# Moving the second half's residual additions behind the numbered rows, and pairing the updates of the third phase

## The chip, the cores and the metric

The program runs on one core of a Trainium2 chip. The metric is the time of one execution in device microseconds; several timed executions are given by their median. The engines are named as in the profile: PE (TensorE), DVE (VectorE), ACT (ScalarE), POOL (GpSimd) and SP (SyncE, which here only issues transfers). Each runs its own instruction list in order, and a semaphore wait in that list holds up everything behind it on that engine.

## The reference, cut to what matters

Eight sequences of 512 tokens with 128 channels go through two layers. The first three blocks (attention, a gated token mix, linear attention with a memory and three MLP levels) take the first 550 us and aren't touched by the change, apart from the residual that they leave in `X`. The change lies in the last block, a router with eight experts and two iterations:

```python
h = layernorm(x)                       # xf below: the block's own input
topk_p, topk_i = top_k(softmax(gelu(xf @ router_w1) @ router_w2), 2)
v, integrated = 0, xf
for _ in range(2):                                   # iterations it = 1, 2
    ctx = concat([integrated, v])
    x_sh, v_sh = _inl(gelu(ctx @ shared_w1) @ shared_w2, integrated, v, mu)
    x_r, v_r = sum over the 2 chosen experts of topk_p * _inl(gelu(ctx @ w1[e]) @ w2[e], ...)
    x_next, v_next = sw * x_sh + (1 - sw) * x_r, sw * v_sh + (1 - sw) * v_r
    integrated = integrated + halt * (x_next - integrated)
    v = v + halt * (v_next - v)
refined = gelu(integrated @ refine_w1) @ refine_w2
out = x + (xf + integration_weight * refined)        # the residual of this block
```

The two additions of the last line are where `X` comes in: the kernel adds the normed input to the residual early (`X += xnb`), and the refined part at the end.

## The kernel before, in words

**Tiles and halves.** A token tile is 128 tokens by 128 channels; a sequence has four. Sequences 0 to 3 are half 0, sequences 4 to 7 half 1. `xnb[t]` is the normed input of sequence t, `Y1[t]` is `xnb[t] - mu`, and `X` is the residual. For half 0 `xnb` lies in `LX`, for half 1 in 2,048 columns of `TEMP` that the expert inputs `XS` use later.

**Routing by slots.** After the router, a half's tokens are sorted by expert into 40 tiles of slots (`sort(h)` on DVE, 20-odd small instructions; its last, line 1123, counts `so_pos`). POOL then writes each token row twice, once for each of its two experts, to the slots in DRAM, with indirect DMAs of 128 rows. For half 0 that is `scatter(0, m)`: 32 DMAs on line 675. For half 1 the rows carry a number in a 129th column, so these 32 DMAs are the numbered rows (`numbered(k, m)`, line 684): 16 for the first expert, a wait and a small instruction, 16 for the second. The first of them waits for `so_pos`; later ones wait for `v_el`, the count of groups that DVE has finished, at values that lag behind the rows.

**Groups.** The iterations run as 56 groups of 512 tokens or slots. An S group is the shared path of four token tiles, an E group the expert path of four slot tiles. The order is S 0 to 3 (half 0, iteration 1), E 4 to 13 (the same), S 14 and 15 and E 16 to 25 (half 1, iteration 1), S 26 and 27, S 28 to 31 and E 32 to 41 (half 0, iteration 2), S 42 to 45 and E 46 to 55 (half 1, iteration 2). Every engine loops over steps s. In step s DVE copies the gate values of group s out of PSUM (`copy_b`, line 1180), runs `elements(s - 2)` (for an S group lines 1211, 1213, 1215, 1222) and `moved_on(s - 2)` (lines 1235, 1244, 1249), and in some steps `routes`, `hots` (line 1081) or `sort` of half 1: routes(1) and hots(1) in step 2, sort(1) in step 3. The E groups of a half and iteration can only be loaded by SP (line 510) when all the rows of that half have landed in the slots.

**Updates.** What an E group gives is stored by slot. POOL gathers it back by token: `gather(ph, m)`, two indirect DMAs on line 770 into one of four buffers `G`, for the 16 tiles m of phase ph (0: half 0, 1: half 1 of iteration 1; 2: half 0 of iteration 2). DVE adds it to the tokens: `update(ph, m)`, lines 1273 and 1276, in a step that the table `UPDATES` gives. `gather(ph, m)` waits for `update(ph, m - 4)`, whose buffer it takes. In the third phase, ph 2, POOL runs step by step too: it first writes the results of E group s - 2 to their tokens (`slots_back`, four indirect DMAs on line 693, three for the last group; they wait for `v_el`), then issues `gather(2, m + 4)` for each update m that the table has for this step. So the table sets DVE's order and POOL's at once.

**The end.** When the last `slots_back` rows have landed, SP reads the rows of half 1 back (`load_tokens`, line 529), DVE makes the updates of phase 3, and PE, ACT and DVE refine the last sequences.

**Around the change.** POOL's list before the numbered rows is: 32 scatter DMAs, then `moved(1)`, which makes the four `Y1` subtractions of half 1 (line 659), the four additions `X += xnb` of half 1 (line 661) and a copy of the row numbers (line 663), then `ones_row(1)`, a memset of one partition (line 699). The same `moved(0)` runs earlier for half 0.

## Time and profile before

| | us |
|---|---|
| timed runs | 991.86, 994.6, 995.5 |
| median | 994.6 |
| the profiled execution | 991.68 |
| its span, first to last instruction | 989.9 |
| PE busy | 782.1 (79%) |
| DVE busy | 577.9 (58%) |
| ACT busy | 566.4 (57%) |
| POOL busy | 488.1 (49%) |

The 1.8 us between the profiled execution and its span lie around the instructions. The shares of busy time are averages over stages with different limits, so they don't say what a change in one stage is worth. For that one follows the chain of waits: the work that ended last, traced back step by step to what released it.

### The profile page before, as it was taken

The page shows a single profiled execution, that of the slowest core. Times are in us where ns is not written, and L with a number is a line of the kernel's source. Part 1 is how long each engine was busy: PE and PEld are TensorE (multiplying, and loading weights), DVE is VectorE, ACT ScalarE, POOL GpSimd, SP SyncE. Part 2 cuts the span into 40 slices and gives each one's busy share as a digit, 9 for nine tenths or more (in the row PEclk, how much of TensorE's full clock was granted, in tenths as well). Part 3 has the DMA queues.
Part 4 walks back from the last instruction along what each step waited for, and adds up shares of the span by engine and source line. Part 5 has one row for each costly group of instructions (what it writes and reads, how often), then busy time and mean ns, then how long its engine had stood idle before and what let it go on. Part 6 is the DMA issues. An engine that isn't in the chain of part 4 may idle for free.

```text
span 989.9 us, 13034 instructions
## 1 busy us (share of the span) xinstructions
PE 782.1 (79%) x3904; PEld 535.8 (54%) x3904; DVE 577.9 (58%) x1438; ACT 566.4 (57%) x1003; POOL 488.1 (49%) x436
## 2 busy tenths in 40 slices
PE   7799997587888877999999856575576668877477
PEld 4588886444444435767676644454344444544255
DVE  6622333648888682222434588658566877586655
ACT  5744444544445304635544539877666898788532
POOL 1411202335554486224434777537777775467750
PEclk9999999799999997999999969887898999888789
DMA  9940000000000000000000535657557664633124
GB/s 344 423 136 1 0 1 1 1 1 0 1 1 1 0 1 0 1 1 1 1 1 27 186 92 152 207 158 226 166 175 238 202 191 146 196 121 101 48 78 128
DMA packets 75921, 92.90 MB, mean 94 GB/s; under 512 B 24032, under 2 KB 61920, under 8 KB 73808
## 3 DMA queue, kind: packets, MB, share of 16 engines
q1 hardware_dynamic: 65248, 65.87, 20.7%
q0 software_dynamic: 10464, 25.66, 8.1%
q10 hardware_dynamic: 144, 0.59, 0.2%
q8 instruction: 31, 0.51, 0.2%
q14 instruction: 34, 0.28, 0.1%
HBM read 45.95 MB, written 46.13 MB: 93 GB/s over the span
## 4 chain that ended last, share of the span: by engine, by line
PE 46%; DVE 16%; POOL 11%; ACT 11%; issue 9%; DMA 5%; POOLq 0%; DVEq 0%; SPq 0%; ACTq 0%
PE PS L1945 7%; PE PS L1954 6%; POOL tokens L693 4%; POOL KEEP L770 3%; PE PS L1752 3%; PE PS L1723 3%; PE PS L1864 3%; PE PS L1960 3%; PE PS L1832 3%; POOL slots L684 3%; PE PS L1713 2%; DMA KEEP<-moved,small 2%; DVE TEMP L961 2%; PE PS L1660 2%; PE PS L2058 2%
## 5 line engine op out<-in xcount | busy, mean ns | idle before, releaser
L2069 PE MATMUL PS<-TEMP,KEEP 128*128 x320 | 116.9, 508 | 36.9 <-ACT TEMP L1569 30.4
L770 POOL DMA_INDIRECT KEEP<-moved,small x96 | 104.4, 1087 | 69.9 <-issue 35.4
L675 POOL DMA_INDIRECT slots<-KEEP,small x96 | 101.1, 1053 | 47.2 <-issue 27.4
L2069 PEld LDWEIGHTS PS<-TEMP,KEEP 128*128 128x128 f32 x320 | 66.5, 223 | 65.1 <-issue 50.7
L1509 ACT ACTIVATE KEEP<-PS,TEMP 128x512 f32<-128x512 f32 x96 | 63.5, 690 | 58.0 <-PE PS L1945 57.1
L1569 ACT ACTIVATE TEMP<-PS 128x512 f32<-128x512 f32 (+2 forms) x92 | 51.5, 561 | 78.3 <-DVE TEMP L1180 77.7
L621 POOL TENSOR_TENSOR KEEP<-KEEP 128x1024 f32<-128x1024 f32 x32 | 63.7, 2005 | 53.6 <-PE PS L1864 51.8
L1945 PE MATMUL PS<-TEMP_R 128*128 128x512 f32 x288 | 77.1, 422 | 4.2 <-POOL TEMP_R L715 3.8
L2091 PE MATMUL PS<-KEEP,TEMP 128*64 128x128 f32 x480 | 40.2, 308 | 42.2 <-issue 19.1
L1864 PE MATMUL PS<-KEEP,TEMP 128*128 128x512 f32 x128 | 62.7, 619 | 9.3 <-DVE TEMP L961 8.2
L1945 PEld LDWEIGHTS PS<-TEMP_R 128*128 128x128 f32 x288 | 56.2, 198 | 20.1 <-POOL TEMP_R L715 4.2
L1180 DVE COPY TEMP<-PS 128x256 f32<-128x256 f32 (+1 forms) x92 | 43.8, 477 | 37.9 <-PE PS L2058 19.4
L2091 PEld LDWEIGHTS PS<-KEEP,TEMP 128*64 128x64 f32 x480 | 29.7, 154 | 64.4 <-issue 25.3
L1582 ACT ACTIVATE KEEP<-PS,TEMP 64x128 f32<-64x128 f32 x160 | 57.7, 360 | 9.4 <-PE PS L2091 7.6
L1954 PE MATMUL PS<-KEEP,TEMP 128*128 128x512 f32 x128 | 56.3, 593 | 0.0
L2058 PE MATMUL PS<-WL,KEEP 128*128 128x257 f32 (+1 forms) x128 | 47.7, 510 | 6.4 <-ACT TEMP L1569 6.3
L1666 PE MATMUL PS<-WL,TEMP 128*128 128x128 f32 x256 | 39.9, 297 | 16.0 <-DMA TEMP<-slots 13.1
L1273 DVE SCALAR_TENSOR_TENSOR KEEP<-KEEP,small 128x256 f32<-128x256 f32 (+1 forms) x64 | 26.5, 414 | 39.7 <-DMA KEEP<-moved,small 33.5
L1127 DVE TENSOR_SCALAR TEMP_R<-PS,TEMP 128x512 fp32r<-128x512 f32 x16 | 12.0, 751 | 62.3 <-PE PS L1954 62.3
L961 DVE TENSOR_TENSOR TEMP<-PS,KEEP 128x1024 f32<-128x1024 f32 x32 | 38.9, 1216 | 15.0 <-PE PS L1864 13.1
L1666 PEld LDWEIGHTS PS<-WL,TEMP 128*128 128x128 f32 x256 | 31.6, 151 | 27.8 <-issue 21.0
L715 POOL TENSOR_TENSOR TEMP_R<-KEEP,TEMP_R 128x512 fp32r<-128x512 f32 x8 | 8.7, 1090 | 73.3 <-ACT KEEP L1501 73.3
(275 smaller groups left out, 1877.5 us busy)
## 6 DMA issues: line engine op xcount, KB each, us to landing
slots<-LX SPq DMA_DIRECT2D x14, 1024.0 KB, 25.8
moved<-LX SPq DMA_DIRECT2D x20, 512.0 KB, 3.3
TEMP<-slots SPq DMA_DIRECT2D x20, 512.0 KB, 3.8
TEMP<-experts SPq DMA_DIRECT2D x80, 64.5 KB
TEMP<-seconds SPq DMA_DIRECT2D x1, 3072.0 KB
TEMP<-early SPq DMA_DIRECT2D x1, 2765.0 KB, 12.0
TEMP<-experts SPq DMA_DIRECT2D x80, 32.5 KB
TEMP<-slots SPq DMA_DIRECT2D x10, 258.0 KB, 3.8
```

Of the source, the lines that this page charges most:

```text
L621: pool.tensor_tensor(o, kk, vv, ALU.mult).then_inc(S["c1_kv"], 1)
L675: pool.indirect_dma_start(dst, bass.IndirectOffsetOnAxis(ap=pos[:, h, 2 * m + k:2 * m + k + 1], axis=0), src, None).then_inc(SC[h], 16)
L770: pool.indirect_dma_start(G[:, n % 4, k, 0:w], None, src, bass.IndirectOffsetOnAxis(ap=pos[:, h, 2 * m + k:2 * m + k + 1], axis=0))\
L961: dve.tensor_tensor(qm[:, c % 2].rearrange("p (h v k) -> p h v k", h=HEADS, v=HD), acc, q, ALU.mult)\
L1509: act.activation(d_G[:, k, SEQ * c:SEQ * (c + 1)], PS[:, 2 + c, :], ACT.Gelu_apprx_tanh, bias=bias)\
L1666: last = pe.transpose(PS[:, bank, P * j:P * (j + 1)], src[:, j], eye)
L1864: last = pe.matmul(PS[:, 4 + 2 * (c % 2) + h, :], we("tril"), kv[:, c % 2, SEQ * h:SEQ * (h + 1)], start=True, stop=True)
L1945: last = pe.matmul(PS[:, 2 + c, :], CWr[:, pw, at:at + P], hTr[:, k, px], start=n == 0, stop=n == 2)
L1954: last = pe.matmul(PS[:, 6 + k, :], w2[:, P * c:P * (c + 1)], d_G[:, k, SEQ * c:SEQ * (c + 1)], start=c == 0, stop=c == HC - 1)
L2058: last = pe.matmul(PS[:, bank + j, 0:n], HS[:, hs_slot(g), col:col + P], wl("sw2")[:, 0:n], start=True, stop=True)
L2069: last = pe.matmul(o, hT[:, e % 3, P * j:P * (j + 1)], EW2[:, 384 * (j % 2):][:, bass.ds(at[j], n)], start=True, stop=True)
L2091: last = pe.matmul(PS[side:side + EHID, bank, part], W1[:, e % 4, j, 1 + EHID * a:1 + EHID * (a + 1)], xTs[:, x % 2, a, part], start=a == ...
```

## The change

Two edits, with what belongs to the first. POOL's four additions `X += xnb` of half 1 leave `moved(1)` and come as `added(1)` behind the last numbered row; those of half 0 stay where they were. Since `xnb` of half 1 must live longer, it moves from `TEMP` to a part of `YV2` that is free until group 14 is moved on; SP's load of the fifth E group then no longer waits for the three counts of that buffer's readers, and DVE's `elements` of an S group in iteration 1 waits for the additions of its half (`r_xa`). The second edit is one table entry: in the third phase update m goes to step 45 + m // 2 instead of 45 + (m + 1) // 2.

```diff
-        UPDATES.setdefault(_at + ((_m + 1) // 2 if _ph == 2 else UPDATE_STEPS[_m]), []).append((_ph, _m))
+        UPDATES.setdefault(_at + (_m // 2 if _ph == 2 else UPDATE_STEPS[_m]), []).append((_ph, _m))
...
-        xnb_1 = TEMP[:, 8 * SEQ:12 * SEQ].rearrange("p (a j d) -> p a j d", a=HSEQ, j=TILES)
+        xnb_1 = YV2[:, HT:HT + 8].rearrange("p (a b) (c d) -> p a (b c) d", a=HSEQ, c=2)
...
-                if e == 4:
-                    sp.wait_ge(S["r_y"], NSEQ)
-                    sp.wait_ge(S["r_xa"], NSEQ)
-                    sp.wait_ge(S["r_tr"], NSEQ)
...
-                for t in range(HSEQ * half, HSEQ * (half + 1)):
-                    pool.tensor_tensor(tiles(X, t), tiles(X, t), xnb[t], ALU.add).then_inc(S["r_xa"], 1)
+                if half == 0:
+                    added(0)
                 if half == 1:
                     pool.tensor_copy(Y1I[:, HT:2 * HT, P], wl("ids")).then_inc(S["p_set"], 1)
                 pool.wait_ge(S["r_y"], HSEQ * (half + 1))
-                pool.wait_ge(S["r_xa"], HSEQ * (half + 1))
                 if half == 1:
                     pool.wait_ge(S["p_set"], 7)
+
+            def added(half):
+                for t in range(HSEQ * half, HSEQ * (half + 1)):
+                    pool.tensor_tensor(tiles(X, t), tiles(X, t), xnb[t], ALU.add).then_inc(S["r_xa"], 1)
+                pool.wait_ge(S["r_xa"], HSEQ * (half + 1))
...
                     need(pool, S["v_el"], (3 * m // 4 + 3 * HT // 4 * k) // 2 - 1)
                     numbered(k, m)
+            added(1)
...
                 if kind == "S" and it == 1:
                     dve.wait_ge(S["r_y"], t + 1)
+                    dve.wait_ge(S["r_xa"], HSEQ * (h + 1))
```

On POOL, around the numbered rows, the list before reads as follows. `slots_0` and `slots_1` are the slots of the two halves, `KEEP` holds `Y1`, `YV2` and the gather buffers, `WL` constants, and a semaphore in brackets is what the instruction waits for.

```order
L675 DMA slots_0<-KEEP,small 5120x128 x31
L659 TENSOR_TENSOR KEEP<-TEMP,WL 128x4x128 [waits r_xn] x4
L661 TENSOR_TENSOR X<-X,TEMP 128x512 x4
L663 COPY KEEP<-WL 128x16
L699 MEMSET KEEP 1x2048 [waits c3_xb,p_set,r_l,r_xa,r_y]
L684 DMA slots_1<-KEEP,small 5120x129 [waits r_one,so_pos]
L684 DMA slots_1<-KEEP,small 5120x129 x5
...
L684 DMA slots_1<-KEEP,small 5120x129 [waits v_el] x15
L770 DMA KEEP<-moved_0,small 128x256 [waits y_out1,y_out0,r_one]
```

The same place now (lines of the changed kernel: 655 is the subtraction, 666 the addition, 659 the copy, 771 the gather):

```order
L675 DMA slots_0<-KEEP,small 5120x128 x31
L655 TENSOR_TENSOR KEEP<-KEEP,WL 128x4x128 [waits r_xn] x4
L659 COPY KEEP<-WL 128x16
L699 MEMSET KEEP 1x2048 [waits c3_xb,r_l,p_set,r_y]
L684 DMA slots_1<-KEEP,small 5120x129 [waits r_one,so_pos]
L684 DMA slots_1<-KEEP,small 5120x129 x5
...
L684 DMA slots_1<-KEEP,small 5120x129 [waits v_el] x15
L666 TENSOR_TENSOR X<-X,KEEP 128x512 x4
L771 DMA KEEP<-moved_0,small 128x256 [waits y_out0,y_out1,r_one,r_xa]
```

The four additions have moved past the copy, the memset and all 32 numbered rows, to just ahead of the first gather of phase 0.

On POOL in the third phase, the list before, from the first gather of phase 2 to the last `slots_back` row (`moved` is what the E groups stored, `tokens` the rows written back):

```order
L770 DMA KEEP<-moved,small 128x128 x18
L693 DMA tokens<-KEEP,small 9216x128 x4
L770 DMA KEEP<-moved,small 128x128 x4
...
L770 DMA KEEP<-moved,small 128x128 x4
L693 DMA tokens<-LX,small 9216x128 x4
L770 DMA KEEP<-moved,small 128x128 x2
L693 DMA tokens<-KEEP,small 9216x128 x8
L693 DMA tokens<-LX,small 9216x128 x8
L693 DMA tokens<-KEEP,small 9216x128 x7
```

And now:

```order
L771 DMA KEEP<-moved,small 128x128 x20
L693 DMA tokens<-KEEP,small 9216x128 x4
L771 DMA KEEP<-moved,small 128x128 x4
...
L771 DMA KEEP<-moved,small 128x128 x4
L693 DMA tokens<-LX,small 9216x128 x4
L693 DMA tokens<-KEEP,small 9216x128 x8
L693 DMA tokens<-LX,small 9216x128 x8
L693 DMA tokens<-KEEP,small 9216x128 x7
```

One gather of two DMAs has moved from between the fourth and the fifth `slots_back` to ahead of the first.

On DVE, the end of step 45 and the start of step 46, before:

```order
L1246 SCALAR_TENSOR_TENSOR KEEP<-KEEP,small 128x128 x3
L1273 SCALAR_TENSOR_TENSOR KEEP<-KEEP,small 128x128 [waits g_in0,v_el]
L1276 SCALAR_TENSOR_TENSOR KEEP<-KEEP,small 128x128 [waits v_up]
L1180 COPY TEMP<-PS 128x256 [waits p_q]
L1211 TENSOR_SCALAR small<-TEMP,small 128x4 [waits a_t,a_l]
```

And now, with the lines of the changed kernel:

```order
L1248 SCALAR_TENSOR_TENSOR KEEP<-KEEP,small 128x128 x3
L1275 SCALAR_TENSOR_TENSOR KEEP<-KEEP,small 128x128 [waits g_in0,v_el]
L1278 SCALAR_TENSOR_TENSOR KEEP<-KEEP,small 128x128 [waits v_up]
L1275 SCALAR_TENSOR_TENSOR KEEP<-KEEP,small 128x128 [waits g_in1,v_el]
L1278 SCALAR_TENSOR_TENSOR KEEP<-KEEP,small 128x128 [waits v_up]
L1181 COPY TEMP<-PS 128x256 [waits p_q]
```

Update 1 has moved from step 46 to step 45, ahead of the copy that opens step 46; each odd update after it has moved up by a step likewise, and step 53, which held update 15 alone, has none.

## Rows read from the trace of the kernel before

**Rows 1.** The page: the chain's shares by line, and the gathers' landing time.
```profile
PE 46%; DVE 16%; POOL 11%; ACT 11%; issue 9%; DMA 5%; POOLq 0%; DVEq 0%; SPq 0%; ACTq 0%
...
KEEP<-moved,small POOLq DMA_INDIRECT x96, 3.1
```

**Rows 2.** Timeline of POOL before the numbered rows: start, us, instruction [idle before].
```profile
571.07 4.94 POOL L659 TENSOR_TENSOR KEEP<-TEMP,WL 128x512 f32<-128x512 f32 x4
575.97 5.63 POOL L661 TENSOR_TENSOR X<-X,TEMP 128x512 f32<-128x512 f32 x4
581.55 0.67 POOL L663 COPY KEEP<-WL 128x16 f32<-128x16 f32 x1
582.42 1.80 POOL L699 MEMSET KEEP<- 1x2048 f32 x1 [0.20 <-issue]
...
589.72 1.00 POOL L684 DMA_INDIRECT slots<-KEEP,small  x1 [5.50 <-DVE small L1123]
```

**Rows 3.** Timeline of DVE in steps 2 and 3.
```profile
565.78 0.22 DVE L1211 TENSOR_SCALAR small<-TEMP,small 128x4 f32<-128x4 f32 x1
...
570.10 0.28 DVE L1065 TENSOR_TENSOR KEEP<-PS,WL 128x128 f32<-128x128 f32 x1
...
576.08 1.43 DVE L1081 TENSOR_TENSOR KEEP<-WL,small 128x256 bf16<-128x256 f32 x1
...
577.77 0.89 DVE L1211 TENSOR_SCALAR small<-TEMP,small 128x4 f32<-128x4 f32 x1
...
583.11 1.14 DVE L1244 SCALAR_TENSOR_TENSOR KEEP<-LX,small,KEEP 128x128 f32<-128x128 f32 x4
...
584.77 0.16 DVE L1088 COPY KEEP<-PS 128x8 f32<-128x8 f32 x1
...
587.34 0.41 DVE L1106 TENSOR_TENSOR TEMP<-TEMP,KEEP 128x256 f32<-128x256 f32 x1
```

**Rows 4.** Timeline of PE: the rank matmuls of half 1.
```profile
577.76 3.75 PE L1998 MATMUL PS<-KEEP 128*128 128x256 bf16 x32
```

**Rows 5.** Timeline of PE: its first turn of group 16.
```profile
643.72 1.08 PE L1666 MATMUL PS<-WL,TEMP 128*128 128x128 f32 x4 [7.09 <-DMA TEMP<-slots]
```

**Rows 6.** Timeline of POOL: the last numbered row and the first gather.
```profile
636.60 1.09 POOL L684 DMA_INDIRECT slots<-KEEP,small  x1 [0.30 <-issue]
657.11 1.45 POOL L770 DMA_INDIRECT KEEP<-moved,small  x1 [19.42 <-DMA moved<-LX]
```

**Rows 7.** Timeline of DVE: the elements of group 14.
```profile
656.73 0.23 DVE L1211 TENSOR_SCALAR small<-TEMP,small 128x4 f32<-128x4 f32 x1 [2.75 <-ACT LX L1560]
```

**Rows 8.** Timeline of SP: its load of the first E group.
```profile
572.39 0.59 SPq L510 DMA_DIRECT2D TEMP<-slots  x1
```

**Rows 9.** Timeline of POOL in the third phase.
```profile
853.95 2.02 POOL L770 DMA_INDIRECT KEEP<-moved,small  x1 [0.30 <-issue]
...
872.17 0.94 POOL L770 DMA_INDIRECT KEEP<-moved,small  x1 [8.60 <-DVE KEEP L1273]
...
922.86 1.31 POOL L770 DMA_INDIRECT KEEP<-moved,small  x1 [0.30 <-issue]
...
925.73 1.00 POOL L693 DMA_INDIRECT tokens<-KEEP,small  x1 [0.30 <-issue]
...
936.89 0.96 POOL L693 DMA_INDIRECT tokens<-LX,small  x1 [0.30 <-issue]
...
955.66 0.96 POOL L693 DMA_INDIRECT tokens<-KEEP,small  x1 [0.30 <-issue]
```

**Rows 10.** Timeline of DVE in the third phase.
```profile
862.37 0.42 DVE L1180 COPY TEMP<-PS 128x256 f32<-128x256 f32 x1 [2.18 <-PE PS L2069]
...
871.17 0.35 DVE L1273 SCALAR_TENSOR_TENSOR KEEP<-KEEP,small 128x128 f32<-128x128 f32 x1
...
930.85 0.69 DVE L1235 SCALAR_TENSOR_TENSOR LX<-TEMP,LX 128x512 f32<-128x512 f32 x1
```

**Rows 11.** Timeline of PE at the end: the turn of the fifth refined sequence.
```profile
963.17 1.08 PE L1666 MATMUL PS<-WL,KEEP 128*128 128x128 f32 x4 [4.41 <-DVE KEEP L1276]
```

## The prediction, made before the changed kernel ran

> **What bounds the kernel now.** I first read the chain of waits by engine and line [rows 1]: no engine carries even half of the span, so the bound differs by stage, and the two places of the change have to be read by themselves. I then read the timelines of all engines at these two places.
>
> Before group 16 everything waits for POOL's numbered rows. PE sits idle for 7.09 us until the load of group 16 has come in [rows 5], and that load is released by the last numbered row's landing; the row was issued at 636.60 [rows 6]. The rows follow one another from 589.72 on with the usual 0.30 us between them. The chain names a DVE group behind the seventh of them, but the code asks there for one finished group, which step 2 had given by 570.10 [rows 3]; the row simply follows the one before. So the end of this stage is set by the start of the rows, and the first row waited 5.50 us for DVE's last sort instruction, line 1123 [rows 2]. POOL itself was ready long before; that its additions leave is worth nothing on POOL. It counts on DVE, which was working towards the sort beside them.
>
> In the third phase POOL is the bound from 872.17 on: every row after it follows the one before by 0.30 us, up to the last one at 955.66, and PE's turn of the fifth refined sequence waits behind that [rows 9, 11]. Ahead of 872.17 POOL sits idle for 8.60 us, until update 1 is made.
>
> **First edit: what it takes off DVE.** The additions run from 575.97 for 5.63 us [rows 2]. DVE's line 1211 takes 0.89 us beside them and 0.22 us in step 2, where POOL only issues rows [rows 3]. So POOL's arithmetic holds DVE up. From the start of line 1211 to the instruction behind the last one of `moved_on`, the same work takes 570.10 - 565.78 = 4.32 us in step 2 and 584.77 - 577.77 = 7.00 us in step 3 [rows 3]: 2.68 us come back. Ahead of it line 1081 takes 1.43 us. A two-input DVE instruction of 128x256 takes 0.41 us alone (line 1106). The copy of 0.67 us now starts where the additions did, at about 576.0; if it holds line 1081, this ends at 576.0 + 0.67 + 0.41 = 577.1 and 0.4 us come back, if not, at 576.5 and 1.0 us [rows 2, 3]. I take 0.4, since the copy is there first and line 1211 shows a DVE instruction held by POOL. Together 3.1 us.
>
> The memset of 1.80 us now runs from about 576.9 to 578.7, beside lines 1211 to 1222 instead of lines 1235 to 1249. Beside it line 1244 took 1.14 us for four, with no sign of a hold [rows 2, 3]. By this row, the nearest, I take 0. The other end: line 1211, due at 577.4, waits until 578.7 and costs about 1.2 us.
>
> PE could take the bound over, since the sort also needs the rank matmuls, which run for some 4.0 us behind line 1081 (the row of 3.75 us ends at 581.51) [rows 3, 4]. They move with it: from 577.1 they end at 581.1, and DVE is there at 584.77 - 3.1 = 581.7. Still DVE, by 0.6 us. The sort itself runs with POOL idle in both kernels and keeps its length.
>
> So the first row starts at 586.6, and the load of group 16, PE's turn and all that follows come 3.1 us earlier; the idle 7.09 us of PE [rows 5] shows that no engine but the load was late there. The rows' own waits for finished groups move along, because DVE's groups start from the same sort.
>
> **First edit: what it adds.** The four additions, 5.63 us, now stand behind the last row, at about 634.9 to 640.5. POOL's next work is the gather, before which it sat idle for 19.42 us [rows 6]; 5.6 fit in it, and without that cover they would cost all 5.6. Their new waiter is DVE's `elements` of group 14 at 656.73 - 3.1 = 653.6 [rows 7], 13 us later. Queued behind that wait on DVE are the updates of phase 0, and on POOL behind the additions the gathers, so both covers must last, and do. DVE's groups 12 and 13 run beside the additions and may lose up to the 2.7 us that step 3 lost; the turn of group 16 waits for a load and not for them. SP's three dropped waits gain nothing: its first E group's load went out at 572.39 [rows 8], and the fifth comes three groups behind that, when POOL had given its counts. Price 0.
>
> **Second edit.** Update 1 moves ahead of the copy that opens step 46, before which DVE waits 2.18 us for PE [rows 10]. An update takes two instructions of 0.35 us, some 0.7 together. Its gather was issued at 853.95 and held POOL until 855.97; with the median landing of 3.1 us from issue it is in by about 858, and even 3.1 us from the end of that long issue gives 859 [rows 1, 9]. So it costs DVE nothing, and up to 2.2 us if that cover weren't there.
>
> Then gather 5 needs no wait for step 46: its two rows fit into the idle 8.60 us. POOL's next gather still waits for step 46's first update, which is at 871.17 as before [rows 10], and starts at 872.17 as gather 5 did. From there POOL's list is the same up to 922.86, with each gather's number one higher. There two rows are missing: the next `slots_back` starts at 922.86 instead of 925.73 [rows 9], 2.87 us earlier. All that follows is back to back, unless a wait opens. The tightest is the `slots_back` of group 52, due at 936.89 - 2.87 = 934.0; it needs DVE's line 1235 of that group, 930.85 + 0.69 = 931.5, and DVE gets there earlier now, since step 53 has no update [rows 9, 10]. Slack 2.5 us. At the end PE's turn waits 4.41 us for DVE [rows 11], more than 2.87, so the tail follows. Taken: 2.87; the low end is 2.5, two rows at 0.96 + 0.30.
>
> **Sum.** 3.1 + 2.9 = 6.0 us. The profiled execution, 991.68 with its span of 989.9, becomes 985.7. It lies 2.9 us under the median of the runs shown, which is what I predict against: 994.6 - 6.0 = 988.6. With the ends of the unknown terms (memset 0 to 1.2, line 1081 0.4 to 1.0, rows 2.5 to 2.87) both edits give 4.4 to 6.6.
>
> **Rivals.** (1) The memset holds line 1211: 6.0 - 1.2 = 4.8, 989.8. For it: a one-tensor DVE instruction was held by POOL here. Against it: line 1244 beside this very memset. The Trainium skill, SBUF — State Buffer, section "Who interferes with whom", has a rule for it: a POOL instruction that only writes doesn't hold up a DVE instruction with two inputs, but it does hold one that uses both ports for a single tensor, as a tensor_scalar may. By that, line 1244 proves nothing for line 1211, and the edit is worth 1.2 us less; the trace has no such instruction beside a memset.
>
> (2) One of the two gains is taken back. In the third phase a wait of POOL for DVE's groups opens, since the slack is only 2.5 us: then 3.1 alone, 991.5. Or DVE's step 3 was late for another reason than the additions, so that the edit doesn't do what it can: 2.9 alone, 991.7. Against both: the rows above.
>
> (3) Slower: the last numbered rows don't land until POOL is done with the additions. A row lands some 3.1 us from its issue, so 2.0 from its end [rows 1, 6]: 639.7 before, and 634.9 + 5.63 + 2.0 = 642.5 then, 2.8 later instead of 3.1 earlier; with the second edit's 2.9 that is no change. If DVE's groups stretch each addition by one more 0.69 us, it is 2.8 + 2.8 - 2.9 = 2.7 slower, 997.3. It decides from additions of over 5.7 us. Against it: half 0's rows, whose last were followed by the subtractions from 571.07 to 576.0, and whose first load went out at 572.39 [rows 2, 8].
>
> **How the numbers follow.** Forecast 0.45, memset 0.27, one gain lost 0.23, slower 0.05. The range 985.5 to 992.3 holds the first two with their ends and most of the third, from the lowest run less 6.4 to the median less 2.3. About 0.5%, 5.0 us, is what a measurement of this kernel can tell from no change. The forecast is mostly beyond it, memset just short of it, one gain within it: faster 0.55, same 0.40, slower 0.05.
>
> **What would show it.** After: DVE's line 1211 of step 3 (1213 there) back at 0.2 us and the sort's first instruction at about 581.7; the first numbered row at about 586.6; PE's idle before the turn of group 16 still some 7 us. In the third phase two more gather rows ahead of POOL's idle stretch, and POOL without a wait behind it. I am wrong if the additions' removal leaves step 3 at 7.0 us, if POOL shows a wait for DVE behind the missing pair, or if the load of group 16 comes after the additions.

## The result and the profile after

The changed kernel took 987.5 us in the median of 16 runs, the kernel before 994.9 in the 16 beside it: a ratio of 0.9925 (0.9906 to 0.9945), or 7.4 us less (5.5 to 9.4). In a second set, with twelve runs of the changed kernel, it was 987.1 us and a ratio of 0.9949 (0.9929 to 0.9970), by that ratio 5.1 us less. The forecast was 988.6, or 6.0 us less. The profiled execution has a span of 983.1 us, against 989.9.

The changed kernel's code stands one or two lines further down on DVE, PE and ACT than that of before (1213 is 1211, 1217 is 1215, 1082 is 1081, 1181 is 1180 and so on). On POOL 655 is the subtraction, 666 the addition, 659 the copy, 771 the gather. The execution after runs 1.4 us later already at step 2, ahead of the change (566.82 against 565.44), so times are compared from there on. The instruction that they are compared from, before:

```profile
565.44 0.42 DVE L1180 COPY TEMP<-PS 128x256 f32<-128x256 f32 x1 [4.87 <-PE PS L2058]
```

The chain on the page after: POOL's share has gone from 11% to 8% [rows 1].

```profile
PE 46%; DVE 17%; ACT 12%; issue 9%; POOL 8%; DMA 6%; SPq 0%; POOLq 0%; DVEq 0%; ACTq 0%
```

DVE's timeline in steps 2 and 3, to be read against [rows 3]:

```profile
566.82 0.42 DVE L1181 COPY TEMP<-PS 128x256 f32<-128x256 f32 x1 [4.87 <-PE PS L2060]
...
577.46 0.42 DVE L1082 TENSOR_TENSOR KEEP<-WL,small 128x256 bf16<-128x256 f32 x1
...
578.14 1.34 DVE L1213 TENSOR_SCALAR small<-TEMP,small 128x4 f32<-128x4 f32 x1
578.26 1.22 DVE L1215 SCALAR_TENSOR_TENSOR small<-TEMP,small 128x4 f32<-128x4 f32 x2
578.41 1.07 DVE L1217 SCALAR_TENSOR_TENSOR TEMP<-TEMP 128x512 f32<-128x512 f32 x1
...
582.87 0.16 DVE L1089 COPY KEEP<-PS 128x8 f32<-128x8 f32 x1
```

Line 1082 takes 0.42 us where 1081 took 1.43. Line 1213 takes 1.34: it is held until the memset ends (below). But the instructions of the two lines behind it start while it is held, and all end together at 579.48, so from 1213's start to line 1089 it is 582.87 - 578.14 = 4.73 us: 7.00 before, 4.32 in step 2 of the kernel before [rows 3].

POOL's timeline from the copy to the first gather, against [rows 2, 6]:

```profile
577.33 0.21 POOL L659 COPY KEEP<-WL 128x16 f32<-128x16 f32 x1
577.65 1.80 POOL L699 MEMSET KEEP<- 1x2048 f32 x1
587.83 1.00 POOL L684 DMA_INDIRECT slots<-KEEP,small  x1 [8.37 <-DVE small L1124]
...
634.31 1.09 POOL L684 DMA_INDIRECT slots<-KEEP,small  x1 [0.31 <-issue]
635.42 4.92 POOL L666 TENSOR_TENSOR X<-X,KEEP 128x512 f32<-128x512 f32 x4
655.03 1.41 POOL L771 DMA_INDIRECT KEEP<-moved,small  x1 [14.69 <-DMA moved<-LX]
```

From step 2's copy to the first numbered row it is 587.83 - 566.82 = 21.01 us. Before it was 589.72 - 565.44 = 24.28. SP's and PE's timelines show what hangs on the last row: the load of group 16 (the second row is the same load before) and PE's turn [rows 5]:

```profile
638.08 1.88 SPq L506 DMA_DIRECT2D TEMP<-slots  x3
```

```profile
640.34 1.87 SPq L510 DMA_DIRECT2D TEMP<-slots  x3
```

```profile
641.34 1.09 PE L1668 MATMUL PS<-WL,TEMP 128*128 128x128 f32 x4 [7.01 <-DMA TEMP<-slots]
```

The load goes out while the additions still run (to 640.34), and PE's turn comes 3.8 us earlier against step 2. DVE's timeline beside the additions shows their cost there; the last row is from the kernel before:

```profile
636.63 4.27 DVE L1217 SCALAR_TENSOR_TENSOR TEMP<-TEMP 128x512 f32<-128x512 f32 x1 [1.74 <-ACT TEMP L1562]
...
644.17 0.42 DVE L1181 COPY TEMP<-PS 128x256 f32<-128x256 f32 x1 [1.62 <-PE PS L2060]
```

```profile
646.56 0.42 DVE L1180 COPY TEMP<-PS 128x256 f32<-128x256 f32 x1 [5.28 <-PE PS L2058]
```

One instruction of group 12, of 0.69 us elsewhere, is held until the fourth addition is done. DVE's idle time ahead of the copy that opens group 16's step shrinks to 1.62 us (before 5.28). POOL in the third phase, against [rows 9], and PE's last turn [rows 11]:

```profile
868.86 0.94 POOL L771 DMA_INDIRECT KEEP<-moved,small  x1 [4.14 <-DVE KEEP L1275]
...
949.24 0.96 POOL L693 DMA_INDIRECT tokens<-KEEP,small  x1 [0.30 <-issue]
```

```profile
957.29 0.63 PE L1668 MATMUL PS<-WL,KEEP 128*128 128x128 f32 x4 [2.02 <-DVE KEEP L1278]
```

POOL's idle stretch shrinks from 8.60 to 4.14 us, and from its end to the last row it is 80.38 us instead of 83.49.

### The profile page after: what moved, and what is told of

It is laid out like the page before. It is cut to its first block, busy times and chain, and to the rows that moved or that the text cites. A ratio compares the mean times of both kernels' runs of the same rounds, so it can differ in the third digit from the quotient of the medians.

```text
span 983.1 us, 13042 instructions
## 1 busy us (share of the span) xinstructions
PE 779.2 (79%) x3904; PEld 534.5 (54%) x3904; DVE 577.9 (59%) x1438; ACT 567.1 (58%) x1003; POOL 489.5 (50%) x436
## 4 chain that ended last, share of the span: by engine, by line
PE 46%; DVE 17%; ACT 12%; issue 9%; POOL 8%; DMA 6%; SPq 0%; POOLq 0%; DVEq 0%; ACTq 0%
PE PS L1947 7%; PE PS L1956 6%; POOL tokens L693 3%; PE PS L1754 3%; PE PS L1725 3%; PE PS L1866 3%; DMA KEEP<-moved,small 3%; PE PS L1962 3%; PE PS L1834 3%; PE PS L1715 3%; POOL slots L684 2%; DVE TEMP L962 2%; PE PS L1662 2%; POOL KEEP L771 2%; ACT L1556 2%
## 5 line engine op out<-in xcount | busy, mean ns | idle before, releaser
L771 POOL DMA_INDIRECT KEEP<-moved,small x96 | 108.5, 1130 | 59.0 <-issue 35.0
L962 DVE TENSOR_TENSOR TEMP<-PS,KEEP 128x1024 f32<-128x1024 f32 x32 | 38.9, 1217 | 14.9 <-PE PS L1866 13.1
L1866 PEld LDWEIGHTS PS<-KEEP,TEMP 128*128 128x128 f32 x128 | 22.6, 194 | 40.1 <-issue 30.9
```

Source lines behind the costliest of these rows:

```text
L771: pool.indirect_dma_start(G[:, n % 4, k, 0:w], None, src, bass.IndirectOffsetOnAxis(ap=pos[:, h, 2 * m + k:2 * m + k + 1], axis=0))\
L962: dve.tensor_tensor(qm[:, c % 2].rearrange("p (h v k) -> p h v k", h=HEADS, v=HD), acc, q, ALU.mult)\
L1866: last = pe.matmul(PS[:, 4 + 2 * (c % 2) + h, :], we("tril"), kv[:, c % 2, SEQ * h:SEQ * (h + 1)], start=True, stop=True)
```

## The experiments

Three stretches are measured in every trace, each from start to start: from step 2's copy on DVE to the first numbered row (A), from the last numbered row to SP's load of group 16 (B), and from POOL's first gather behind step 46 to the last `slots_back` row (C). The ratios are to the kernel before, with 95% intervals.

| kernel | A | B | C | ratio (95%) |
|---|---|---|---|---|
| before | 24.28 | 3.74 | 83.49 | 1 |
| changed | 21.01 | 3.77 | 80.38 | 0.9925 (0.9906 to 0.9945) |
| changed, second set | 20.99 | 8.54 | 80.28 | 0.9949 (0.9929 to 0.9970) |
| first edit alone | 20.99 | 3.66 | 83.59 | 0.9954 (0.9931 to 0.9978) |
| second edit alone | 24.28 | 3.76 | 79.84 | 0.9964 (0.9941 to 0.9986) |
| additions ahead of the rows | 25.25 | 3.70 | 80.57 | 0.9975 (0.9950 to 1.0001) |
| memset later (first try) | 21.70 | 3.75 | 80.61 | 0.9952 (0.9928 to 0.9976) |
| memset later (second try) | 21.09 | 2.65 | 79.95 | 0.9953 (0.9929 to 0.9978) |
| additions twice | 21.01 | 3.85 | 80.33 | 0.9907 (0.9884 to 0.9930) |
| subtractions earlier | 18.65 | 11.32 | 80.37 | 1.0003 (0.9981 to 1.0024) |
| three updates | 21.01 | 3.84 | 77.37 | 0.9896 (0.9870 to 0.9922) |
| three updates, second set | 21.00 | 4.00 | 77.76 | 0.9912 (0.9887 to 0.9938) |
| three, additions wait | 21.00 | 3.69 | 78.41 | 0.9904 (0.9869 to 0.9940) |

The kernel with four updates has no idle stretch from which C could be counted and stands in the last section of this part.

### Each edit alone

The first edit alone is the changed kernel with the old table:

```diff
-        UPDATES.setdefault(_at + (_m // 2 if _ph == 2 else UPDATE_STEPS[_m]), []).append((_ph, _m))
+        UPDATES.setdefault(_at + ((_m + 1) // 2 if _ph == 2 else UPDATE_STEPS[_m]), []).append((_ph, _m))
```

> The changed kernel with the old table of updates: the first edit alone. Theory (the two edits are worth about 3.5 and 3.1 us, and add up): about 3.5 us under the kernel before; the first numbered row starts at 587.8 to 588, PE's turn of group 16 comes 2 to 4 us earlier than before's 643.72, while POOL again idles some 8 us ahead of its fifth gather of the third phase and its rows up to the last slots_back keep the old length of 83.5 us from there. Rival (the whole gain is the second edit's, and the first edit's is given back before the end): within 1 us of the kernel before. Rival (the whole gain is the first edit's): 6 to 7 us under it.

The second alone is the kernel before with the opposite line.

> The kernel before with only the new table of updates: the second edit alone. Theory: about 3 us under the kernel before (2.9 to 3.1 by the two rows that leave POOL's back-to-back stream). Everything up to the third phase stands as before (first numbered row at about 589.7, turn of group 16 at about 643.7); in the third phase POOL's idle stretch shrinks from 8.6 to about 4.1 us and the stream behind it from 83.5 to about 80.4 us. Rival (the gain there came from the higher granted clock that the changed kernel's trace shows around 850): POOL's stream is still shorter, but the span gains under 1.5 us.

The table shows them apart: A shortens by 3.3 us with the first edit alone and not with the second, C by 3.1 us (3.65 in the second edit's own trace) with the second and not with the first. In time they are 4.6 and 3.6 us under the kernel before, each with 2.3 us to either side, so the sum of 8.2 fits the 7.4 and the 5.1 of both together. Both rivals, that one edit carries all, fall. C holds two rows fewer by its definition; that is a gain because its start isn't later for it: 21.31 us behind the phase's first gather with the first edit alone, 21.46 with the second, 21.45 with both. Before it was 22.59, in a trace whose granted clock from 850 to 875 us is 0.82, where it is 0.93 in these three. The clock, the rival of the second expectation, doesn't make the gain in C: with the first edit alone it is 0.93 too, and C kept its length. POOL's timeline of the first alone shows the idle stretch still long, 6.75 us in this execution, and the old C:

```profile
864.93 0.94 POOL L771 DMA_INDIRECT KEEP<-moved,small  x1 [6.75 <-DVE KEEP L1275]
...
948.52 0.96 POOL L693 DMA_INDIRECT tokens<-KEEP,small  x1 [0.30 <-issue]
```

### Is it the arithmetic beside DVE, or POOL's place in the list?

```diff
                 pool.memset(HS[96:97, HSEQ * h:HSEQ * (h + 1)], 1.0).then_inc(S["r_one"], 1)
+                if h == 1:
+                    pool.wait_ge(S["r_one"], 2)
+                    added(1)
                 pool.wait_ge(S["so_pos"], h + 1)
...
-            added(1)
```

> The changed kernel, but POOL makes the four additions right behind the memset, ahead of the numbered rows, inside its idle stretch of 8.37 us before the first row. They fit there (4.9 to 5.6 us), so POOL's own list is not late. Theory (POOL's arithmetic beside DVE is what the move takes away): DVE's stretch from line 1213's start in step 3 to the instruction behind moved_on grows again from 4.73 us to between 6 and 7 us, or the sort's first instructions do by as much; the first numbered row comes 1.3 to 2.7 us later than in the changed kernel, and the time is 1 to 3 us over it. Rival (what counts is POOL's place in the list, or the buffer that moved): no change to the changed kernel, first row at 587.8.

DVE's timeline of this kernel (four lines lower on DVE than before: 1226 is the group's `TENSOR_TENSOR` 1222, 1248 the four of 1244) and the first row on POOL:

```profile
579.38 1.79 DVE L1226 TENSOR_TENSOR LX<-TEMP,KEEP 128x512 f32<-128x512 f32 x1
...
582.89 3.04 DVE L1248 SCALAR_TENSOR_TENSOR KEEP<-LX,small,KEEP 128x128 f32<-128x128 f32 x4
```

```profile
591.88 1.01 POOL L684 DMA_INDIRECT slots<-KEEP,small  x1 [6.61 <-issue]
```

POOL ends its additions 6.6 us ahead of that row, so they aren't late in its list, and yet A is 25.25 us, even longer than before. Line 1226 takes 1.79 us in place of 0.69, line 1248 3.04 for four in place of 1.14. The theory holds and its size was too small (4.2 us later than in the changed kernel, 1.3 to 2.7 expected; half a microsecond of the 4.2 lies behind the sort, see the memset below): the additions hold DVE's lines there as they held others in the kernel before. The rival falls by A; the time, 0.9975, can't be told from the changed kernel's.

### What is left beside DVE: the memset

The memset of half 1 is moved behind the sixteenth numbered row, where POOL waits for landings anyway; the first row then waits for the sort and, in the first try, for half 0's memset too, which is long done.

```diff
                 if k == 1 and m == 0:
+                    ones_set(1)
                     pool.wait_ge(SC[1], 16 * HT)
...
             def ones_row(h):
+                if h == 0:
+                    ones_set(0)
+                pool.wait_ge(S["so_pos"], h + 1)
+                pool.wait_ge(S["r_one"], 1)
+
+            def ones_set(h):
```

> The changed kernel with the one-partition memset of half 1 moved behind the first sixteen numbered rows, into a stretch in which POOL waits some 3.5 us for their landing anyway. Theory (the memset holds line 1213, but the instructions behind it overlap with the hold, so that it costs some 0.4 us and not 1.1): line 1213 of step 3 is back at 0.22 us, the stretch up to the instruction behind moved_on goes from 4.73 to about 4.3 us, the first numbered row comes 0.4 us earlier, and the time is the changed kernel's within what can be measured. Rival (the whole hold is on the path): 1.1 us earlier. Rival (line 1213 is held by something else, the copy of the row numbers or the operands that it waits for): it stays over 1 us.

This couldn't tell: the last scatter rows came late in this trace, the subtractions ended 12.06 us behind step 2's copy in place of 10.57, and they held line 1213 (0.90 us) in the memset's place. The second try drops the wait on `r_one`:

> The changed kernel with half 1's memset behind the first sixteen numbered rows, and the first row waiting for the sort alone. In the earlier kernel with the memset there, the scatter rows ahead of the subtractions came 1.3 us later than in every other run, so that the subtractions held line 1213 instead, and the row started 0.57 us later behind the sort. Theory (the memset's hold costs 0.4 us of DVE's time, since what follows overlaps): if the subtractions end at their usual place, line 1213 takes 0.22 us, the stretch from there to the instruction behind moved_on is 4.3 us instead of 4.73, and the first numbered row starts 20.6 us behind step 2's copy instead of 21.0. Rival (the whole 1.1 us of the held instruction are on the path): 19.9 us. If the subtractions come late again, it can't be told, and the row is where it was.

Here the subtractions end where they did in the changed kernel. DVE's timeline (1218 is 1213, 1094 is 1089) and the first row:

```profile
579.56 0.22 DVE L1218 TENSOR_SCALAR small<-TEMP,small 128x4 f32<-128x4 f32 x1
...
583.87 0.15 DVE L1094 COPY KEEP<-PS 128x8 f32<-128x8 f32 x1
```

```profile
589.32 1.00 POOL L685 DMA_INDIRECT slots<-KEEP,small  x1 [10.36 <-DVE small L1129]
```

The held instruction is free (0.22 us), and the stretch is 583.87 - 579.56 = 4.31 us, as in step 2. So the memset's hold costs 4.73 - 4.31 = 0.42 us, not the 1.1 that the held instruction shows. Still A is 21.09, where 20.6 was expected: the sort ends at 588.53 and the row starts 0.79 us later, where it is 0.28 in the changed kernel. In the two other kernels in which something else than the memset was POOL's last instruction ahead of the rows it is 0.85 (first try) and 0.76 (additions ahead of the rows). What costs that half microsecond stays open. In time nothing is won.

### What is left beside DVE: the subtractions

```diff
             for m in range(HT):
+                if m == 11:
+                    moved(1)
                 scatter(0, m)
-            moved(1)
             ones_row(1)
```

> The changed kernel with POOL's four subtractions and the copy of the row numbers of half 1 made ahead of the last ten scatter rows of half 0 instead of behind them, at about 558 to 563 in the trace, where DVE mostly waits for PE. Theory (DVE in step 3 is still held by the subtractions, whose end at 577.39 is where its cast of 1.30 us ends): cast and line 1075 of step 3 take 0.2 us each as in step 1, the sort ends some 2 us earlier and the first numbered row starts some 2 us earlier. For the time two outcomes: the price is that half 0's last rows land 5 us later, and with them the E groups 4 and 5; the numbered rows wait for finished groups (one at 600.61 starts right when group 4 is finished), so the gain is kept only if group 4 isn't late: between 2 us faster and 3 us slower than the changed kernel. Rival (step 3 is late for another reason): the first numbered row stays at its place against step 2.

DVE's timeline (1078 is the cast of step 3, 1214 is 1213), and POOL's and SP's:

```profile
575.64 0.18 DVE L1078 CAST small<-KEEP 128x32 f32<-128x32 uint32 x1
...
576.53 0.22 DVE L1214 TENSOR_SCALAR small<-TEMP,small 128x4 f32<-128x4 f32 x1
...
636.78 5.27 DVE L1218 SCALAR_TENSOR_TENSOR TEMP<-LX,TEMP 128x512 f32<-128x512 f32 x1 [0.34 <-ACT LX L1563]
```

```profile
585.79 0.96 POOL L684 DMA_INDIRECT slots<-KEEP,small  x1 [3.96 <-DVE small L1125]
602.73 0.97 POOL L684 DMA_INDIRECT slots<-KEEP,small  x1 [3.26 <-DVE KEEP L1252]
```

```profile
643.54 0.33 SPq L523 DMA_DIRECT2D moved<-LX  x1
646.38 0.43 SPq L523 DMA_DIRECT2D moved<-LX  x1
646.92 2.04 SPq L506 DMA_DIRECT2D TEMP<-slots  x3
```

With no POOL work beside it but scatter rows and, at 580.03, the memset, DVE's step 3 runs free (from 1214 to the instruction behind `moved_on` it is 4.32 us, as in step 2), and A falls by another 2.36 us to 18.65. So POOL's arithmetic made the step late: 3.3 us of it the additions, 2.4 the subtractions, the copy and the memset beside line 1213. The price eats it: half 0's groups come late, the numbered rows wait for them (3.26 us at 602.73), and in the end group 16's load goes out 11.32 us behind the last row, since it stands on SP behind the stores of groups 10 and 11 (643.54, 646.38), and the additions had held group 10 on DVE for 5.27 us. The time is that of the kernel before.

### How much cover the additions' new place has

Four more additions behind the four, whose sums aren't used:

```diff
             added(1)
+            for t in range(HSEQ, NSEQ):
+                pool.tensor_tensor(xnb[t], tiles(X, t), xnb[t], ALU.add).then_inc(S["r_xa"], 1)
+            pool.wait_ge(S["r_xa"], NSEQ + HSEQ)
...
-                    dve.wait_ge(S["r_xa"], HSEQ * (h + 1))
+                    dve.wait_ge(S["r_xa"], (HSEQ, NSEQ + HSEQ)[h])
```

> The changed kernel with four further additions of the same size behind the four on POOL, whose sums nobody reads: the cover of the additions' new place doubled in cost, 9.8 us in place of 4.92. Theory (DVE's line 1217 of group 12 is held as long as the train of additions lasts, and DVE had only 1.62 us of idle time left there): that instruction takes 4.27 + 4.9 = 9.2 us, DVE's idle stretch behind it is gone, and the copy of group 16's first step (644.17 in the changed kernel) and the first gather behind come 2 to 3.5 us later, the time 2 to 3.5 us over the changed kernel; that would mean that the new place had 1.6 us of cover left and not the 14 us of POOL's idle time. Rival (the hold ends with the first few additions, or POOL's idle time alone is the cover): copy and first gather stay where they are and the time is the changed kernel's.

DVE's timeline (1220 is 1217, 1227 is 1224), and POOL's second train and first gather:

```profile
639.10 4.26 DVE L1220 SCALAR_TENSOR_TENSOR TEMP<-TEMP 128x512 f32<-128x512 f32 x1 [1.74 <-ACT TEMP L1565]
643.39 1.64 DVE L1227 TENSOR_TENSOR LX<-TEMP 128x512 f32<-128x512 f32 x1
```

```profile
642.88 6.64 POOL L764 TENSOR_TENSOR KEEP<-X,KEEP 128x512 f32<-128x512 f32 x4
657.24 0.99 POOL L774 DMA_INDIRECT KEEP<-moved,small  x1 [7.72 <-DMA moved<-LX]
```

My theory fell. The first four hold one instruction to their end, but between the two trains, at POOL's own wait, DVE gets in, and beside the second train it loses 0.6 to 1.0 us for each of four instructions. The first gather stands 13.31 us behind PE's turn of group 16 (657.24 - 643.93), against 13.69 in the changed kernel, and the time, 0.9907, isn't longer. In this alignment, with the rows ending where group 12 begins on DVE, the place has cover for twice the work.

### The changed kernel once more, and the cover broken

> The changed kernel once more, beside the next two, to compare them under one set of runs: 0.99 to 0.995 of the kernel before, with the first numbered row 21.0 us behind the copy that opens step 2, and POOL's third-phase stream 80.4 us long from the end of its 4.1 us idle stretch.

A and C came as expected. B, of which the expectation says nothing, is 8.54 us in place of 3.77. POOL's, DVE's and SP's timelines of this execution:

```profile
632.92 4.93 POOL L666 TENSOR_TENSOR X<-X,KEEP 128x512 f32<-128x512 f32 x4
```

```profile
632.62 5.80 DVE L1217 SCALAR_TENSOR_TENSOR TEMP<-LX,TEMP 128x512 f32<-128x512 f32 x1
...
639.18 0.69 DVE L1237 SCALAR_TENSOR_TENSOR LX<-TEMP,LX 128x512 f32<-128x512 f32 x1
```

```profile
639.90 0.33 SPq L523 DMA_DIRECT2D moved<-LX  x1
640.34 2.06 SPq L506 DMA_DIRECT2D TEMP<-slots  x3
```

Its numbered rows, the same list, took 44.36 us from first to last in place of 46.48 (the last at 631.80, 634.31 in the first execution). So the additions began 0.30 us behind the start of line 1217 of group 11, not of group 12, and held it. Group 11's store, at 634.76 in the first execution, came at 639.90, and the load of group 16 stands behind that store in SP's list. With B as in the first it would have been at 635.6: 4.8 us lost there, and PE's turn came at 644.05. So at the load of group 16 the additions' new place is free or costs up to 4.8 us, by where in DVE's groups the last row ends. In the table's seven other traces with the additions and the rows at these places B is 2.65 to 4.00. That the loss reaches the end isn't shown: against step 2 the first gather of phase 0 comes 2.8 us later than in the first execution, but the first of phase 2 at the same place (280.55 us, 280.59 there), and the two executions took 984.8 and 984.7 us.

### The additions made to wait

The last experiment has three updates (next section) and one more line:

```diff
                     numbered(k, m)
+            pool.wait_ge(S["v_el"], 14)
             added(1)
```

> Three updates in the third phase's first step, and the four additions now wait until DVE has finished group 13, some 12 us behind the last numbered row. In every trace so far in which they followed that row at once, their train held one instruction of DVE for 4.3 to 5.8 us: line 1217 of group 12 where they began at 634.4 or later, and of group 11 in the second run of the changed kernel, where they began at 632.92; there SP's store of group 11 came at 639.90 in place of 634.76, and the load of group 16 queued behind it. Theory: with the wait the additions run from about 648 to 653, where DVE waits for PE and ACT; line 1217 of groups 11 and 12 takes 0.69 us again, DVE's idle time ahead of the first copy of group 16's step is over 5 us as in the kernel before, the load of group 16 comes some 2 us behind the last row's issue in every execution, and elements of group 14 starts where it did. In an execution like the first ones that is worth nothing (the hold was covered), in one like the second up to 5 us. So the time is that of three updates or up to 1 us less, some 9.5 to 11 us under the kernel before. Rival (the additions' new neighbour, elements of group 14 or the first gather, waits for them now): the first gather or line 1213 of group 14 comes later by what the train overlaps, up to 3 us.

```profile
647.49 4.96 POOL L666 TENSOR_TENSOR X<-X,KEEP 128x512 f32<-128x512 f32 x4 [11.87 <-DVE LX L1238]
654.89 1.49 POOL L772 DMA_INDIRECT KEEP<-moved,small  x1 [2.44 <-DMA moved<-LX]
```

```profile
636.86 0.69 DVE L1218 SCALAR_TENSOR_TENSOR TEMP<-TEMP 128x512 f32<-128x512 f32 x1 [1.73 <-ACT TEMP L1563]
...
644.30 0.42 DVE L1182 COPY TEMP<-PS 128x256 f32<-128x256 f32 x1 [5.09 <-PE PS L2061]
...
654.55 0.23 DVE L1214 TENSOR_SCALAR small<-TEMP,small 128x4 f32<-128x4 f32 x1 [2.86 <-ACT LX L1563]
```

POOL's rows and DVE's: line 1217 (1218 here) of group 12 is back at 0.69 us, DVE's idle time at 5.09 (5.28 before), B is 3.69, and neither the first gather nor `elements` of group 14 waits for the additions. So the place is free in this alignment; that the wait also avoids the late load of the other one is argued from the order, not shown. The time is that of three updates without it.

### How far the table can be driven

Three updates in step 45, then four (with `max(_m, 2) - 2` in place of `max(_m, 1) - 1`):

```diff
-        UPDATES.setdefault(_at + (_m // 2 if _ph == 2 else UPDATE_STEPS[_m]), []).append((_ph, _m))
+        UPDATES.setdefault(_at + ((max(_m, 1) - 1) // 2 if _ph == 2 else UPDATE_STEPS[_m]), []).append((_ph, _m))
```

> The changed kernel with three updates in the third phase's first step instead of two, so that one more gather of two rows stands ahead of POOL's remaining idle stretch of 4.14 us. Theory (the second edit's gain is rows that fit into POOL's idle stretch, and there is room for one more pair): the idle stretch shrinks to about 1.6 us and the back-to-back stream behind it from 80.4 to about 77.9 us; 2 to 2.5 us under the changed kernel, some 9.5 us under the kernel before. Rival (the slack of the slots_back rows is used up: group 52's stand at 930.25 and need what DVE ends at about 926.1): with 2.5 us less the slack is 1.7 us and holds, but if DVE doesn't get earlier too, a wait opens and under 1 us is gained. Rival (the third update delays DVE's step 46, which waits 3.22 us for PE there): step 46 starts up to 0.7 us later, with no gain at the end.

> Three updates in the first step once more. In the run before this one POOL was left without any idle time from 849.44 to the last row, 97.7 us, where the changed kernel took 101.8. If that holds: 2.5 to 4.1 us under the changed kernel in the same set of runs. If the run before was chance, under 1.5 us.

> Four updates in the third phase's first step. Theory (what a pair of rows brings is POOL's idle time that it fills, and with three updates there is none left): POOL's stream from its first gather of the phase to the last row stays at 97.7 us, within 0.5, and the time is that of three updates within 1 us; DVE's step 46 starts some 2.5 us later than with three, since update 3's gather is issued 2.5 us behind update 2's, and it must not matter as long as the slots_back rows have their slack of 3 us. Rival (each pair moved is worth 2.5 us by itself): 2.5 us less again. Rival (the later step 46 reaches the slots_back rows): a wait of POOL for DVE in the stream and 0.5 to 2 us more.

POOL's timeline with three updates, in the second set:

```profile
869.29 0.94 POOL L771 DMA_INDIRECT KEEP<-moved,small  x1 [1.28 <-DVE KEEP L1275]
...
947.05 0.95 POOL L693 DMA_INDIRECT tokens<-KEEP,small  x1 [0.31 <-issue]
```

Another pair of rows leaves the stream, C is 77.37 and 77.76 us, and the idle stretch is 0.30 (none) and 1.28. Beside the changed kernel in one set it is 983.85 us (six runs) against 987.14 (twelve); in its two sets it is 10.3 and 8.7 us under the kernel before. So it beats both kernels. The gain isn't the same in every execution: with the additions made to wait, PE was 1.46 us late for DVE's step 45, the idle stretch was 3.54 and C 78.41.

With four updates POOL has no idle time at all from its first gather on (843.87) to the last row (942.56). That is 98.69 us, where three took 97.73 and 98.74 (101.38 with the additions made to wait) and two 101.83 (98.99 to 102.92 over the eight traces with two). DVE waits 4.51 us for the gather of update 2, 3.77 with three. The ratio is 0.9900 (0.9868 to 0.9931), not to be told from three, and not precise enough to refute the rival of another 2.5 us. So by POOL's stream a pair is worth 2.5 to 3 us as long as POOL has idle time for it, and nothing after; the second half of that rests on one trace.

## Why the prediction was right, point by point

**The sum, 6.0.** A and C together give 3.27 + 3.11 = 6.4 us; the two sets give 7.4 and 5.1. The mechanism of both edits is the one that was forecast. That the first edit's term came out so close is in part luck, and one step, the additions' new place at nothing, failed in part, as said below.

**What bounds, and that only the start of the rows counts.** Right. POOL waits 8.37 us for the sort where it waited 5.50, PE's idle time before its turn is 7.01 us (forecast some 7), and the rows keep their pace.

**Step 3 of DVE, 2.68 back.** 2.27 came back. The missing 0.4 is the memset, which I had put at 0 from line 1244's row. Rival 1's mechanism is real: line 1213 is held to the memset's end, at the other end of the bound. The Trainium skill, SBUF — State Buffer, section "Who interferes with whom", says that a POOL instruction that only writes doesn't contend with a DVE instruction of two inputs, but that a one-tensor instruction that uses both ports contends with POOL. The row of 1.34 us agrees. But the price is 0.42 us by the memset experiment and not 1.2: I had charged the whole hold of one instruction to the path, and the three instructions behind it start before it ends.

**Line 1081, 0.4 back.** 1.0 came back, the bound's other end: the copy takes 0.21 us where it had taken 0.67, and line 1082 beside its end isn't held. The two errors cancel by luck: 3.27 us in A, 3.1 forecast.

**PE's rank matmuls.** Right that DVE stays last. They end at about 581.4, DVE is there at 582.87.

**The additions' new place, 0.** This step failed in part. The two covers that I named, POOL's idle time and the 13 us to DVE's waiter, both held. I wrote that groups 12 and 13 may lose time and that the turn of group 16 waits for a load and not for them. But on SP the load stands behind the store of group 11, and when the rows end early the additions hold that group: the load came 4.8 us late in one of two profiled executions of this kernel. I had followed POOL's and DVE's lists behind the moved step and left out SP's. I also had the hold too small, 2.7 us by step 3's loss, where one instruction alone lost 3.6 to 5.1. Rival 3 named the right victim, the load of group 16, by a wrong way: the rows' landing isn't delayed by the additions (the load goes out at 638.08 beside them).

**SP's dropped waits, 0.** Nothing in the traces speaks against it. The kernel with the additions ahead of the rows has dropped them too: against the second edit alone its A is 1.0 us longer and its time 1.1 us (0.9975 and 0.9964), so they have nothing to show, as far as times known to 2.3 us can tell.

**The second edit, 2.87.** 3.11 by C, 3.65 in its own trace, none with the first edit alone. Update 1 cost DVE nothing: its copy of step 46 still waits 3.22 us for PE. No wait opened in POOL's stream. The slack of group 52's rows, 2.5 us by forecast, was 4.2 (930.25 less 926.05, the end of DVE's line 1237), as DVE got earlier too. The tail gave back half a microsecond: from the last row to PE's turn it is 8.05 us, 7.51 before. The rows that show the two covers, on DVE and on POOL:

```profile
860.75 0.42 DVE L1181 COPY TEMP<-PS 128x256 f32<-128x256 f32 x1 [3.22 <-PE PS L2071]
...
925.36 0.69 DVE L1237 SCALAR_TENSOR_TENSOR LX<-TEMP,LX 128x512 f32<-128x512 f32 x1
```

```profile
930.25 1.22 POOL L693 DMA_INDIRECT tokens<-LX,small  x1 [0.30 <-issue]
```

**Rival 2.** Refuted by the two edits alone: each is faster than the kernel before, clear of no change, and no wait of POOL opened.

## What to carry to other kernels

Arithmetic on POOL can cost DVE time where the two overlap, so move it to where DVE waits, not to where POOL does. If that place drifts between executions, a wait for a DVE event pins it. When a held engine feeds a store, follow the queue that issues the store: what stands behind it there is late too, even if it needs nothing of it. A held instruction's own duration is no price, since its successors may have started; measure from its start to an instruction some way behind.

## What the runs showed of the hardware that I had not expected

- A train of POOL's additions, back to back, holds one two-input DVE instruction to its end (4.27 us beside 4.92 of additions; 5.80 in the other alignment, where by the trace that instruction had started 0.30 us ahead of them), and POOL loses nothing. The Trainium skill, SBUF — State Buffer, section "Who interferes with whom", calls the ports that DVE shares with POOL an exclusive lock and says, where it speaks of DVE's two-port modes, that the one that issues first gets them for the whole instruction. Here, with a DVE instruction of two inputs, POOL kept them for four instructions. In the kernel before POOL's additions took 5.63 us and DVE got in between them [rows 2, 3].
- Four DVE instructions in a row, the held one and those of lines 1215 and 1217 behind it, start within 0.27 us and end together when the hold ends (579.48).
- Executions differ by up to 3 us, nearly as much as either edit is worth, in a stretch that no edit touches: from the first gather of phase 0 to the first of phase 2 it is 192.47 us before, 192.38 after, 189.99 with the first edit alone and 189.51 in the changed kernel's second trace. That is why every stage had to be read by itself, and why the times of the two edits alone are known to 2.3 us only, while A and C, with the same edits and nothing else changed in their stretches, repeat within 0.1 and 0.8 us.
